# The bank tables of score tiles and of chunks for the maxima are split, their short place lies behind a batch of values, and one division moves ahead of a reduction

## The reference

```
energy = jnp.einsum('bhqd,bhkd->bhqk', q, k)
att = jax.nn.softmax(energy, axis=-1) / D ** 0.5
out = jnp.einsum('bhqk,bhkd->bhqd', att, v)
```

## Time and profile before

| | |
|---|---|
| runs | 2974.85, 2975.08, 2975.32 us |
| median | 2975.08 us |
| profiled execution, its own time | 2976.52 us |
| its span | 2974.7 us |
| mean granted clock of TensorE | 0.969 of full speed |
| busy, TensorE matmul | 2714.5 us, 91% |
| busy, VectorE | 2227.8 us, 75% |
| busy, ScalarE | 1827.2 us, 61% |
| busy, GpSimd | 1986.0 us, 67% |

### The profile page before, as it was taken

How to read it: one execution, slowest core, us unless ns; L and a number is a source line. 1 busy time by engine, 2 the same in 40 slices (tenths; PEclk the granted TensorE clock), 3 DMA queues, 4 the chain that set the end, 5 groups by cost and what they waited for, 6 DMA issues and landing times. The chain is left out here.

```text
span 2974.7 us, 70680 instructions
## 1 busy us (share of the span) xinstructions
PE 2714.5 (91%) x22259; PEld 1500.9 (50%) x22313; DVE 2227.8 (75%) x4482; ACT 1827.2 (61%) x3287; POOL 1986.0 (67%) x1685
## 2 busy tenths in 40 slices
PE   7999899998999989999559998998999899958998
PEld 6655466554755547554235554554455455524444
DVE  4777678776887768777667768777877787728997
ACT  3366555665556654666346676667666766647887
POOL 0298824886268951899428895997799688954441
PEclk9999999999999999999879999999999999969999
DMA  6122343223422424222032214322232232143000
GB/s 213 44 55 54 127 133 104 54 67 125 152 73 54 124 84 147 62 57 82 36 110 71 62 27 115 77 55 54 88 80 56 72 76 55 38 166 127 29 28 36
DMA packets 101850, 243.24 MB, mean 82 GB/s; under 512 B 18620, under 2 KB 24900, under 8 KB 100552
## 3 DMA queue, kind: packets, MB, share of 16 engines
q1 hardware_dynamic: 99784, 233.49, 27.6%
q0 software_dynamic: 1792, 6.33, 0.6%
HBM read 99.15 MB, written 38.88 MB: 46 GB/s over the span
## 5 line engine op out<-in xcount | busy, mean ns | idle before, releaser
L486 DVE TENSOR_REDUCE b_mxs<-ps 128x1 f32<-128x512 f32 x1024 | 640.5, 683 | 182.1 <-PE ps L359 181.9
L486 DVE TENSOR_REDUCE a_mxs<-ps 128x1 f32<-128x512 f32 x1024 | 640.0, 683 | 164.5 <-PE ps L359 164.5
L449 ACT ACTIVATE a_p<-ps 128x512 f32<-128x512 f32 x1024 | 526.3, 603 | 113.0 <-PE ps L373 109.9
L449 ACT ACTIVATE b_p<-ps 128x512 f32<-128x512 f32 x1024 | 525.9, 602 | 88.8 <-PE ps L373 84.9
L329 POOL TENSOR_TENSOR b_sum<-b_p 128x512 f32<-128x512 f32 x384 | 492.8, 1290 | 59.3 <-PE ps L391 47.1
L329 POOL TENSOR_TENSOR a_sum<-a_p 128x512 f32<-128x512 f32 x384 | 496.5, 1300 | 47.0 <-PE ps L391 43.3
L359 PE MATMUL ps<-b_k,b_q 96*128 96x512 f32 x1024 | 450.5, 444 | 30.8 <-DVE b_mxs L486 26.6
L359 PE MATMUL ps<-a_k,a_q 96*128 96x512 f32 x1024 | 426.6, 425 | 7.4 <-DVE a_mxs L486 6.1
L373 PE MATMUL ps<-b_q,b_k 98*128 98x512 f32 x1024 | 403.4, 419 | 16.4 <-ACT b_p L449 6.2
L373 PE MATMUL ps<-a_q,a_k 98*128 98x512 f32 x1024 | 403.7, 417 | 9.9 <-ACT a_p L449 6.4
L334 POOL TENSOR_TENSOR a_sum<-a_sum,a_p 128x512 f32<-128x512 f32 x256 | 332.5, 1299 | 35.5 <-POOL a_sum L329 27.0
(11 more groups left out here) (267 smaller groups left out, 4168.3 us busy)
## 6 DMA issues: line engine op xcount, KB each, us to landing
a_q<-a_qh SPq DMA_DIRECT2D x128, 128.0 KB, 2.3
a_k<-a_kh SPq DMA_DIRECT2D x128, 128.0 KB, 2.3
b_q<-b_qh SPq DMA_DIRECT2D x128, 128.0 KB, 2.3
b_k<-b_kh SPq DMA_DIRECT2D x128, 128.0 KB, 2.4
a_p<-in_w_fc SPq DMA_DIRECT2D x12, 1024.0 KB, 8.1
a_kl<-in_x SPq DMA_DIRECT2D x4, 2048.0 KB, 8.5
a_q<-a_ql SPq DMA_DIRECT2D x64, 128.0 KB, 2.3
a_k<-a_kl SPq DMA_DIRECT2D x64, 128.0 KB, 2.3
```

The source lines that it names most:

```text
L449: act.activation(self.key_tile(u, kt), self.st[RING[CHUNKS * (k % NJ) + n]], ACT.Exp, scale=self.scale).then_inc(self.s_exp, 1)
L486: dve.reduce_max(self.mxs[:, j % 2, c:c + 1], self.mx[RING[CHUNKS * j + c]], axis=AX.X).then_inc(self.s_mxr, 1)
```

## The change

The one table becomes two, one for score tiles (`ST_RING`) and one for chunks (`MX_RING`), each made by a function that is told at which place the turn over the banks slips by one. That place is 30 for score tiles (head 1 modulo 4, tile 14) and 42 for chunks (head 2 modulo 4, chunk 10, which is computed in step 7 of the turns 0, 4, 8, 12). Each table has returns after 2, 4, 2, 4 tiles at its place and the three following, and after 3 elsewhere; the seam from place 63 to 0 has 3. The number of banks, of tiles and their order stay. The credits stay 4.

In `run_dve`, the first division of even heads is issued ahead of both reductions of step 3 rather than between them. That of odd heads stays in step 2 between its two reductions.

```
+def ring(at):
+    return [t % 3 if t < at else (t - (2 if t == at else 1)) % 3 for t in range(NJ * CHUNKS)]
+def back(banks):
+    n = len(banks)
+    return [next(d for d in range(1, n) if banks[(t - d) % n] == banks[t]) for t in range(n)]
+ST_RING, MX_RING = ring(CHUNKS + 14), ring(2 * CHUNKS + 10)
+ST_BACK, MX_BACK = back(ST_RING), back(MX_RING)
...
-        pe.wait_ge(self.s_mxr, CHUNKS * N + c - BACK[at] + 1 + self.MX_CREDIT)
+        pe.wait_ge(self.s_mxr, CHUNKS * N + c - MX_BACK[at] + 1 + self.MX_CREDIT)
...
-        pe.wait_ge(self.s_exp, CHUNKS * N + n - BACK[at] + 1 + self.EXP_CREDIT)
+        pe.wait_ge(self.s_exp, CHUNKS * N + n - ST_BACK[at] + 1 + self.EXP_CREDIT)
...
             for s in range(steps):
                 a = 1 if s < 2 else 2
+                if s == 3 and k % 2 == 0 and ok(k - 1):
+                    self.divide(dve, 2 * N - 2, 0, 4 * i + k - 1)
                 for c in range(2):
                     if ok(k + a):
                         self.reduce_chunk(dve, N + a, (k + a) % NJ, (2 * s + c + CHUNKS - 4) % CHUNKS)
-                    if s == (2 if k % 2 else 3) and c == 0 and ok(k - 1):
+                    if s == 2 and k % 2 and c == 0 and ok(k - 1):
                         self.divide(dve, 2 * N - 2, 0, 4 * i + k - 1)
```

More of the change, by code:

```diff
@@ L42 @@
 CHUNKS = 16
-RING = [t % 3 for t in range(60)] + [0, 1, 2, 1]
-BACK = [next(d for d in range(1, 64) if RING[(t - d) % 64] == RING[t]) for t in range(64)]
+def ring(at):
[5 more added lines that the diff above has]
+ST_BACK, MX_BACK = back(ST_RING), back(MX_RING)
 LN_EPS, RMS_EPS, Q_EPS = 1e-5, 1e-6, 1e-5
@@ L144 @@
     ST_CREDIT = NJ * CHUNKS
-    EXP_CREDIT = max(BACK)
-    MX_CREDIT = max(BACK)
+    EXP_CREDIT = max(ST_BACK)
+    MX_CREDIT = max(MX_BACK)
     SUM = TT
@@ L356, in max_chunk @@
         at = CHUNKS * j + c
-        pe.wait_ge(self.s_mxr, CHUNKS * N + c - BACK[at] + 1 + self.MX_CREDIT)
+        pe.wait_ge(self.s_mxr, CHUNKS * N + c - MX_BACK[at] + 1 + self.MX_CREDIT)
         t, half = c // 2, c % 2
-        pe.matmul(self.mx[RING[at]], self.q[j][0:96, t * P:(t + 1) * P],
+        pe.matmul(self.mx[MX_RING[at]], self.q[j][0:96, t * P:(t + 1) * P],
                   self.k[j][0:96, half * HALF:(half + 1) * HALF], start=True, stop=True).then_inc(self.s_mx, 1)
@@ L369, in scores @@
         at = CHUNKS * j + n
-        pe.wait_ge(self.s_exp, CHUNKS * N + n - BACK[at] + 1 + self.EXP_CREDIT)
+        pe.wait_ge(self.s_exp, CHUNKS * N + n - ST_BACK[at] + 1 + self.EXP_CREDIT)
         if n == 0:
             pe.wait_ge(self.s_m[j], 16 * (round_ + 1))
-        pe.matmul(self.st[RING[at]], self.k[j][0:98, kt * P:(kt + 1) * P],
+        pe.matmul(self.st[ST_RING[at]], self.k[j][0:98, kt * P:(kt + 1) * P],
                   self.q[j][0:98, u * HALF:(u + 1) * HALF], start=True, stop=True).then_inc(self.s_st, 1)
@@ L448, in exp @@
         act.wait_ge(self.s_pv, self.ROUNDS * M + self.FREED[CHUNKS * ((k - 1) % 2) + n] + 1 + self.PV_CREDIT)
-        act.activation(self.key_tile(u, kt), self.st[RING[CHUNKS * (k % NJ) + n]], ACT.Exp, scale=self.scale).then_inc(self.s_exp, 1)
+        act.activation(self.key_tile(u, kt), self.st[ST_RING[CHUNKS * (k % NJ) + n]], ACT.Exp, scale=self.scale).then_inc(self.s_exp, 1)
     def m_row(self, act, N, j, u):
@@ L485, in reduce_chunk @@
         dve.wait_ge(self.s_mx, CHUNKS * N + c + 1)
-        dve.reduce_max(self.mxs[:, j % 2, c:c + 1], self.mx[RING[CHUNKS * j + c]], axis=AX.X).then_inc(self.s_mxr, 1)
+        dve.reduce_max(self.mxs[:, j % 2, c:c + 1], self.mx[MX_RING[CHUNKS * j + c]], axis=AX.X).then_inc(self.s_mxr, 1)
     def m_parts(self, dve, N, j):
```

## The result

| | before | after |
|---|---|---|
| median of the runs | 2975.2 us | 2948.0 us (2946.7 to 2949.9) |
| ratio | | 0.9907, 95% interval 0.989 to 0.9924 |
| profiled execution, span | 2974.7 us | 2944.9 us |
| mean granted clock | 0.969 | 0.969 |

The runs became 27.2 us shorter where 31.3 us were forecast. Measured again later beside other runs of the kernel before, the changed kernel gave 2946.4 us and a ratio of 0.9891 (0.9874 to 0.9907); the two intervals overlap.

The account below looks back on a forecast made before the run. TensorE is busy 91% of the span, but behind the values VectorE's reductions set the pace. Terms 1.14 + 0.75 + 2.34 - 0.32 = 3.91 us per batch, 31.3 us over eight, give 2975.1 - 31.3 = 2943.8 us; range 2936 to 2963 us.

Parts of the forecast that it names:

- Removed from heads 4, 8, 12: Score tile 1 there no longer waits for an exponential; chunk 1 and the values come 0.38 us sooner, 3 places per batch.
- Heads 2, 6, 10, net of both tables: Waits of chunks 15 and 1 go (0.73 us), score 0 comes 0.48 us later; values 0.25 us sooner per head.
- Added to heads 1, 5, 9, 13: Chunk 12 waits for chunk 10's reduction: 0.08 us lost in 4 heads per batch, bounds nothing and 0.37 us.
- The larger sum: If weight loads were pulled past the waits, each of 8 new places per batch 0.08 to 0.10 us cheaper, some 6 us more.
- The division: Even heads 2 to 12: moved ahead of chunk 2's reduction, reductions behind and values of step 6 0.39 us earlier, 6 per batch.
- Head 14: Chunk 15's wait of 0.49 us goes and 0.48 us come at score 0: nothing in sum.
- POOL: Sums for value rounds 8 to 10 have 0.82 us to spare, 0.38 goes; 1.34 us idleness falls by at most 0.38 + 0.39.
- A: Rival: bank tables bring nothing as POOL's sums or ScalarE become late, the division brings all of its own; 2956.4 us; chance 0.13.
- B: Rival: banks bring their part, division none, as ScalarE's exponentials and TensorE's queue take over the pace; 2962.5 us; chance 0.07.
- D: Rival: no change, the shortened heads only move a wait to something with its own period; 2975 us; chance 0.04.
- C: Rival, slower: the division waits for transposes and blocks VectorE's reductions, 0.60 us late in 48 stretches; 2991.3 us; chance 0.04.
- The signs of being wrong: Values showing new waits for sums, or a head's first score tile waiting over 0.5 us; chunk 15 was to have no wait.

Follow-up runs that it names:

- e3: Kernel before with only the score table changed, table of the maxima and division as before: 2978.3 us, ratio 1.0008 (0.9999 to 1.0017).
- e2: Kernel before with only the table of the chunks for the maxima changed, score table and division as before: 2959.9 us, ratio 0.9948 (0.9934 to 0.9961).
- e1: Kernel before with only the division of even heads moved ahead of chunk 2's reduction, its one table kept: 2952.4 us, ratio 0.9921 (0.9908 to 0.9935).
- e7: As e4, but POOL copies each head's values twice: 2956.6 us, ratio 0.9924 (0.9908 to 0.9941).
- e6: As e4, but the division of even heads one place further ahead, before `m_parts` at the end of step 2: 2953.8 us, ratio 0.9921 (0.9904 to 0.9937).
- e4: Changed kernel, but each table slips by a single repeat lying across a batch of values: 2925.1 us, ratio 0.9825 (0.9812 to 0.9839).

## Why the prediction was right

Direction, mechanism and size came out as forecast, and 2948.0 us lies in the range; the sum was 31.3 us where the loops gave 29.4 us in one execution and 26.3 us in the other, and the runs 27.2 and 33.4 us. In the middle of the loops the sum can be compared like for like: there it stands at 31.3 - 8 x 0.48 = 27.5 us, since the late score 0 of head 14 falls into the middle and what was to make up for it does not. Measured were 26.2 and 26.4 us. By its own steps:

- **Removed from heads 4, 8, 12**, taken as 0.38 us: the values start 3.17 - 2.83 = 0.34 us sooner. This term was a little too large: chunk 1 came 2.45 us after chunk 12, as forecast, but takes 0.45 us, and the values follow it by 0.38 us, not by 0.33 us. Why it takes longer is not shown.
- **Heads 2, 6, 10, net of both tables**, taken as 0.25 us. Score 0 without its wait would start 0.24 us after score 15, at 563.90. It starts at 564.27 and takes 0.10 us longer, so in effect it is 0.47 us late, forecast 0.48 us. Chunk 12 would naturally be at 564.13, and the values start 3.28 us after that, as forecast (571.22 - 567.94), where they took 3.53 us before. The step held, and e3 shows that its reason held too: the delay passes through VectorE's row.
- **Added to heads 1, 5, 9, 13**, taken as 0.08 us: e2 has 0.09 us, and the tile of chunk 12 is 0.10 us back.
- **Weight loads are not pulled ahead of such waits.** Score 0 of head 6 starts with its load and lasts 0.50 us instead of 0.40 us, as does chunk 12 of head 5. Score 15 ahead of it waits for nothing, and its load, at 563.42, starts 0.24 us before its tile, at 563.66, while the tile before is still running. The Trainium skill ("TensorE: Matmul & The Clock Gate", Step-by-step) says that TensorE pulls weight loads ahead of running matmuls; the trace agrees where no wait for a bank stands between, and shows no pull past such a wait. The larger sum that the prediction worked out from that page was rightly not used.
- **The division**, taken as 0.39 us in 48 stretches: the reciprocal starts 0.07 us after the transposes end (forecast 0.08 us), chunk 2's reduction 1.10 us after their start (before 0.94 us, forecast 0.16 us more), and the transposes of step 6 follow 546.24 - 541.59 = 4.65 us after those of step 2 by the timeline of PEld, not 5.04 us as before. That is 0.39 us in head 4; e1 gives 0.35 us as the mean of both layers. The bound of 0.54 us was not reached.
- **Head 14**, taken as nothing: its score 0 starts 0.32 us later, and score 0 to score 6 takes 0.33 us less (5.63 instead of 5.95 us, mean of the eight batches). Heads 0, 14 and 15 together gave 3.2 us in one execution and nothing in another, which the terms don't explain.
- **POOL**, taken to have just room: 0.47 us are left in head 4 and 0.58 us of idleness in an even head. e7 shows that it was no more than that.
- **Rivals.** A falls by e2, B by e1, D by both. C is refuted by e1; e6, where the division does block the row, shows 0.52 us for a stretch where C had 0.60 us. B took ScalarE's exponentials at 0.52 us each; in head 5 of the kernel before, where the loads of scores wait for them, eight in a row took 4.06 us, and one alone takes 0.57 us, which is (4.06 - 0.57) / 7 = 0.50 us each.
- **More banks and another order of banks.** The Trainium skill ("TensorE: Matmul & The Clock Gate", HAM oscillation) reports of another kernel that adding PSUM double-buffering gave no further gain. No run here adds a bank; the order in which three banks come round is changed, and e2 and e4 gain by it.
- **The signs of being wrong.** Two of them were badly chosen. The first score tile of a head was to wait for no more than 0.5 us; its load in head 6 stood for 0.65 us, and that of chunk 15, which was to have no wait, for 0.18 us. By the letter the first of these would have refuted the prediction. But a load's wait is not the delay of its tile, as the prediction says itself: the load of score 1 in the earlier trace rows stood for 0.68 us and cost 0.38 us. And the view of waits puts more loads of values down to sums, 46 and 44 where it was 28 and 29. In heads 1 to 13 none of them stands idle for more than 0.33 us, which such loads do anyway, and all the idle time ahead of loads of values there is the same, 216.7 us before and 216.6 us after: only the name of what ended it changed.

What the prediction did not see is that the change stops halfway. It reckoned the second short return of each table at 0.48 and 0.08 us a place and took it as given that a table of 64 tiles must have two. It need not: e4 has a table with one repeat, and wins another 16.5 us in the middle of the loops.

Nor did it set its own terms for the score table against each other. It wins 3 x 0.38 = 1.14 us in a batch (heads 4, 8, 12) and costs 0.48 us in each of heads 2, 6, 10 and 14, 1.92 us. The gain of heads 2, 6, 10 came from the table of the maxima, and hid that the score table's short place was better off where it had been. e3 and the sum of the three edits show the loss.

## What to carry to other kernels

Where a ring of buffers doesn't divide the loop, the one irregular return should reuse the same buffer on either side of work that uses none of the ring: a return after one step, fully covered, is better than two after two steps of which one is bare. Add up each table by itself before moving both: a gain of one can hide a loss of the other. When an engine sets the pace of a stretch, a side job in its queue belongs into the idle time ahead of the stretch, behind all short work that can fill the wait; one place too early cost 0.52 us here, one too late 0.35 to 0.39 us. Count what the next engine has left before asking for more: here POOL had half a microsecond for a pair of heads.

## What the runs showed of the hardware

The time outside the loops changed by up to 11 us between kernels that have the same instructions there. Part of it goes with TensorE's clock. The three gaps between the loops of the first layer took 128.4, 128.6 and 130.4 us in the profile of before, and 126.1, 125.7 and 127.4 us in e4. In the view by stretch the third number from the right is the granted clock: 0.97, 0.97 and 0.95 in the three gaps of before, 0.99 in all three of e4. TensorE was at its higher level of 2.4 GHz (1.00) for most of a gap and at the lower one of 1.2 GHz (0.50) for a few microseconds. The first and third gap before:

```profile
356.00:484.00 128.00, 117.52 (x544) 82.41 (x544) 97.98 (x183) 59.56 (x94) 29.40 (x26) 0.97 0.42 135
...
1064.00:1195.00 131.00, 120.77 (x548) 84.36 (x544) 98.16 (x181) 59.55 (x94) 29.75 (x26) 0.95 0.40 134
```

and in e4:

```profile
352.00:478.00 126.00, 117.30 (x548) 82.00 (x544) 97.72 (x182) 59.57 (x94) 28.28 (x24) 0.99 0.42 136
...
1048.00:1174.00 126.00, 116.21 (x542) 81.63 (x542) 98.16 (x181) 58.51 (x92) 27.88 (x25) 0.99 0.42 139
```

In the first gap both kernels come to the lower level at the same point of the work, beside a wait of TensorE of 3.9 us for ScalarE. Before, the level holds from 402.5 to 409.3; in e4 it holds only from 399.8 to 403.2. The view by stretch and the timeline of PE, before:

```profile
402.50:409.30 6.80, 4.90 (x12) 3.84 (x13) 6.65 (x11) 4.46 (x8) 1.18 (x1) 0.50 0.82 304
...
404.40 2.07 PE L891 MATMUL ps<-a_h_hi,a_q 128*128 128x512 f32 x4 [3.92 <-ACT a_h_hi L958]
```

and e4:

```profile
399.80:403.20 3.40, 3.40 (x10) 2.63 (x9) 3.25 (x7) 2.13 (x5) 0.00 (x0) 0.50 0.95 366
...
399.36 1.75 PE L906 MATMUL ps<-a_h_hi,a_q 128*128 128x512 f32 x4 [3.93 <-ACT a_h_hi L973]
```

So the gaps are 2 to 3 us longer in the kernel with the lower mean clock. That shorter loops bring this about is not shown: the changed kernel has gaps of 128.9, 130.3 and 128.3 us, at 0.97, 0.95 and 0.97. It stays open how much of the spread of the runs (2971 to 2981 us for the kernel before beside e1 to e4) is due to it. Heads 0, 14 and 15 of the batches spread likewise, between -3.9 and +9.3 us, and the cause was not traced.
